# Two loads of 128 KB for each chunk's up and gate weights, with the down weights' load between them

## The chip, the cores and the metric

The kernel runs on one core of one Trainium2 chip. The metric is the device time of one execution in microseconds (us). Five engines work side by side: TensorE (PE, whose weight loads are shown apart as PEld), VectorE (DVE), ScalarE (ACT), GpSimd (POOL) and SyncE (SP), which here issues nearly all transfers from memory (HBM) to the on-chip SBUF.

## The reference, cut to what matters

The input x has 4 sequences of 512 tokens with 512 features. An attention layer comes first, then a recurrent cell (GRU) over the 512 positions, and its states go through a mixture of experts whose result is added to x:

```
x = x + attention(interpolate(x, cond))
h = cond;  for t in 512 steps:                  # GRU, all four sequences at once
    r, z = sigmoid(x[t] W_ih + h W_hh + b)      # first two thirds
    n    = tanh(i_n + r * h_n);  h = (1 - z) n + z h
for every token (2048) and every expert e (16, plus one shared):
    y += weight[token, e] * ((silu(h w1_e^T) * (h w3_e^T)) w2_e^T)
x = x + y
```

All 16 experts are computed for all tokens; the routing weight is zero for most. With the shared one there are 704 (filled up to 768) + 16 * 352 = 6400 hidden units, which is 50 chunks of 128.

## The kernel before, in words

After the attention, `scan_and_ffn` cuts the 512 positions into `NBLK` = 8 blocks of 64 steps. While the scan runs through block b, the feed-forward of block b-1 (256 tokens) is computed in the time that TensorE would otherwise wait. The feed-forward of the last block has nothing beside it: it is the kernel's tail.

One block's feed-forward has `NCH` = 50 chunks. Across the blocks they are numbered n = 50 f + c, 0 to 399. For each chunk:

- `up(f, c)` (L1235) waits for the chunk's up and gate weights in `w13` and does 16 matmuls (L1242), eight with the w=0 half (up, from w1) and eight with the w=1 half (gate, from w3), each half being 4 slices of 128x128 in bf16, used twice. The last adds one to `up_done`.
- ScalarE, VectorE and GpSimd turn this into the hidden units `hid`.
- `down(f, c)` (L1249) does 8 matmuls (L1257) with the chunk's down weights in `w2`. The last adds one to `down_done`.

TensorE's order is written out by hand: for each of the 64 steps, `scan_step` (96 matmuls, L1207) and then so many units of ups and downs as the tables `UPS`, `DOWNS` and `LEFT` say. In the tail it is up, down, up, down, with the down two chunks behind the up (L1327 to L1331).

Weights come from HBM again for every block. `w13` has two slots, `w2` has twelve. SyncE's program (`chunks`, L852) says in which order loads are issued: for chunk n the load of w13 for chunk n+2 (256 KB, L846, `w13_load`), which waits until up(n) is done since it takes its slot; then w2 for chunk n (128 KB, L850, `w2_load`), which waits until down(n-12) is done; and for every fourth chunk, except in the last two blocks, a load of 128 KB of GRU inputs (L842, `gi_load`). Each DMA adds 16 to its slot's semaphore when it has landed. An engine's program is in order: what stands behind a waiting instruction waits too.

Of the kernel before, what the change touches and what calls it, by code (L numbers as in the profile page):

```python
# [5 lines left out]
P = 128  # L6
# [3 lines left out]
KT = D // P  # L10
# [4 lines left out]
NBLK = S // TB  # L15
TOK = B * TB
SCH = -(-SI // P)
NCH = SCH + E * TOPI // P
# [690 lines left out]
def scan_and_ffn(nc, a, ps, x2T, whh, wih, bias, spare, h, gi_dram):  # L709

    with ExitStack() as ctx:
        def sb(name, shape, dt):
            return ctx.enter_context(nc.sbuf_tensor(name, shape, dt))

        def sem(name):
            return ctx.enter_context(nc.semaphore(name))
# [19 lines left out]
        w13 = sb("w13", [P, 2, 2, KT, P], BF16)  # L736
# [28 lines left out]
        w13_in, w2_in = [sem("w13_in0"), sem("w13_in1")], [sem("w2_in%d" % n) for n in range(W2S)]  # L765
# [21 lines left out]
        def need(eng, sem, count):  # L787
            if count > 0:
                eng.wait_ge(sem, count)
# [41 lines left out]
        @block.sync  # L831
        def _(sp):
            for dst, src in ((gwf[:], a["gate"]), (ne[:], a["ne"]), (identf[:], a["identf"]), (owner[:], a["owner"])):
                sp.dma_start(dst, src).then_inc(init_in, 16)

            def send_gates(j):
                sp.wait_ge(g_out, j + 1)
                sp.dma_start(gi_dram[1 + j // M3, :, j % M3], gis[:, j % GIS].rearrange("p b t -> p (b t)")).then_inc(gi_sent[j % GIS], 16)

            def gi_load(blk, m):  # L840
                sp.wait_ge(h_ready, (blk - 1) * TB + 1)
                sp.dma_start(gi[blk % 2][:, m].rearrange("p b t -> p (b t)"), gi_dram[blk, :, m]).then_inc(gi_in[blk % 2], 16)  # L842

            def w13_load(n):
                need(sp, up_done, n - 1)
                sp.dma_start(w13[:, n % 2], a["w13"][n % NCH].rearrange("p (w k i) -> p w k i", w=2, k=KT)).then_inc(w13_in[n % 2], 16)  # L846

            def w2_load(n):
                need(sp, down_done, n - W2S + 1)
                sp.dma_start(w2[:, n % W2S], a["w2"][n % NCH]).then_inc(w2_in[n % W2S], 16)  # L850

            def chunks(f):  # L852
                for c in range(NCH):
                    n = f * NCH + c
                    if n + 2 < NBLK * NCH:
                        w13_load(n + 2)
                    w2_load(n)
                    if c % 4 == 2 and f + 2 < NBLK:
                        gi_load(f + 2, c // 4)

            w13_load(0)
            w13_load(1)
            for j in range(M3, GATES):
                send_gates(j)
            for n in range(GIS):
                sp.wait_ge(gi_sent[n], 16 * ((GATES - M3) // GIS))
            for f in range(NBLK):
                chunks(f)
            sp.wait_ge(out_done, 16 * NBLK)
# [329 lines left out]
        def _(pe):  # L1199
# [34 lines left out]

            def up(f, c):  # L1235
                n, u = f * NCH + c, c % 2
                pe.wait_ge(w13_in[u], (n // 2 + 1) * 16)
                need(pe, up1_done, n - 1)
                for w in range(2):
                    for k in range(KT):  # L1240
                        for s in range(2):
                            mm = pe.matmul(ps[:, UB[u], w * TOK:(w + 1) * TOK], w13[:, u, w, k],  # L1242
                                           hb[:, f % 2, s, k].rearrange("p b t -> p (b t)"),
                                           start=(w + k + s == 0), stop=(k == KT - 1 and s == 1), skip_group_check=True)
                        if w == 1 and k == KT - 1:
                            mm.then_inc(up_done, 1)
                        yield
# [15 lines left out]
            def all_ups(f):  # L1263
                for c in range(NCH):
                    yield from up(f, c)
# [137 lines left out]
```

## Time and profile before

| what | value |
|---|---|
| runs | 2694.81, 2695.28, 2695.60 us; median 2695.28 |
| profiled execution, its own time | 2695.09 us |
| its span, first to last instruction | 2693.3 us |
| mean granted TensorE clock | 0.984 |
| TensorE busy | 2537.0 us, 94% |
| VectorE, GpSimd, ScalarE busy | 69%, 42%, 40% |
| up and gate weights' loads | 400 of 256 KB, median 2.7 us from issue to landing |
| down weights' loads | 400 of 128 KB, median 2.7 us |
| read from HBM | 185.51 MB, 74 GB/s over the span |

The first load of a chunk's weights to matter is at 858 us, when the first up starts; the stretch from 860 to 2540 us is called the main stretch here (scan and feed-forward together), and from 2543 us to the end it is the tail. "Issue" is the moment at which SyncE starts the DMA instruction, "landing" the moment at which its semaphore is full.

### The profile page before, as it was taken

How to read it: one execution, taken by the hardware profiler on the slowest of the kernel's cores; microseconds unless marked ns; L12 is line 12 of the kernel's file. 1: busy time of each engine (PE TensorE's matmuls, PEld its weight loads, DVE VectorE, ACT ScalarE, POOL GpSimd, SP SyncE). 2: the span in 40 equal slices, each digit the busy share in tenths (PEclk: the TensorE clock that was granted, in tenths of full speed). 3: DMA queues.
4: the chain of work that ended last, by engine and by line, in shares of the span. 5: the costliest groups of instructions: out<-in, count | busy, mean ns of one | idle time of the engine just before them, and what ended most of it. 6: DMA issues, size and time to landing. Idle time of an engine off the chain costs nothing.

```text
span 2693.3 us, 159401 instructions
## 1 busy us (share of the span) xinstructions
PE 2537.0 (94%) x69506; PEld 1989.6 (74%) x69506; DVE 1864.9 (69%) x7035; ACT 1077.3 (40%) x3639; POOL 1142.8 (42%) x2962
## 2 busy tenths in 40 slices
PE   5879797879999999999999999999999999999999
PEld 2334343538888888888888888888888888888888
DVE  4647474635666777787787778777777777878622
ACT  4473736263333333333333333333333333333333
POOL 2504030103333555455455545554554555455454
PEclk9899999999999999999999999999999999999999
DMA  4100000001111333333233323333332333233244
GB/s 170 56 3 18 10 10 3 2 14 39 49 49 56 96 99 93 94 95 98 86 99 99 91 84 108 94 98 94 94 98 81 99 100 94 88 89 89 87 151 133
DMA packets 144746, 209.39 MB, mean 78 GB/s; under 512 B 16432, under 2 KB 86320, under 8 KB 143664
## 3 DMA queue, kind: packets, MB, share of 16 engines
q1 hardware_dynamic: 142896, 195.01, 23.6%
q8 instruction: 546, 8.95, 1.4%
q10 hardware_dynamic: 1152, 4.19, 0.4%
q14 instruction: 152, 1.25, 0.1%
HBM read 185.51 MB, written 13.63 MB: 74 GB/s over the span
## 4 chain that ended last, share of the span: by engine, by line
PE 71%; DVE 3%; POOL 1%; issue 1%; ACT 1%; DMA 0%; DVEq 0%; POOLq 0%; ACTq 0%
PE ps L1207 27%; PE ps L1242 24%; PE ps L1257 12%; PE ps L1219 6%; PE ps L1231 2%; POOL hidf L899 1%; DVE turn_n L1088 0%; DVE turn L1091 0%; DVE fresh L1101 0%; DVE hcur L1103 0%; DVE hcur L1106 0%; DVE npre L1094 0%; DMA w<-in_w 0%; ACT cand L995 0%; DVE h L1104 0%
## 5 line engine op out<-in xcount | busy, mean ns | idle before, releaser
L1207 PE MATMUL ps<-whh,hcur 128*32 128x128 f16 x49152 | 792.5, 220 | 25.7 <-DVE hcur L1106 13.1
L1207 PEld LDWEIGHTS ps<-whh,hcur 128*32 128x32 f16 x49152 | 694.3, 97 | 149.8 <-DVE hcur L1106 119.7
L1242 PE MATMUL ps<-hb,w 128*128 128x256 f16 x6400 | 782.3, 273 | 0.4 <-DMA w<-in_w 0.3
L1242 PEld LDWEIGHTS ps<-hb,w 128*128 128x128 bf16 x6400 | 602.8, 98 | 96.2 <-DMA w<-in_w 1.4
L891 POOL COPY hb<-hcur 128x32 f16<-128x32 f16 x512 | 170.3, 333 | 666.3 <-DVE hcur L1106 666.3
L988 ACT ACTIVATE r<-ur 128x16 f32<-128x16 f32 x512 | 110.6, 216 | 828.6 <-DVE ur L1082 828.6
L1257 PE MATMUL ps<-hid,w 128*128 128x256 f16 x3200 | 428.4, 273 | 2.2 <-POOL hid L911 1.8
L1257 PEld LDWEIGHTS ps<-hid,w 128*128 128x128 bf16 x3200 | 312.4, 98 | 39.7 <-issue 3.0
L899 POOL TENSOR_TENSOR hidf<-up 128x256 f32<-128x256 f32 x400 | 292.1, 730 | 99.1 <-POOL hid L911 50.8
L911 POOL TENSOR_TENSOR hid<-hidf,hid 128x256 f16<-128x256 f32 x400 | 269.5, 674 | 61.8 <-ACT hid L984 61.8
L1079 DVE STREAM_TRANSPOSE turn<-ps 128x128 f32<-128x128 f32 x512 | 161.8, 316 | 180.3 <-PE ps L1207 170.7
L488 DVE TENSOR_REDUCE mx<-ps 128x2 f32<-128x256 f32 (+3 forms) x256 | 197.6, 818 | 63.3 <-PE ps L626 62.4
L990 ACT ACTIVATE z<-uz 128x16 f32<-128x16 f32 x512 | 110.4, 216 | 324.9 <-POOL uz L907 324.9
L1073 DVE TENSOR_TENSOR up<-ps,wsb 128x256 f32<-128x256 f32 x352 | 149.5, 425 | 93.5 <-ACT sg L978 92.1
L405 ACT ACTIVATE stage<-ps,cs 128x1024 f32<-128x1024 f32 (+3 forms) x256 | 186.6, 791 | 42.2 <-PE ps L649 35.2
L905 POOL TENSOR_TENSOR zs<-turn 128x16 f32<-128x16 f32 x512 | 113.3, 221 | 204.8 <-DVE turn L1084 201.1
L1088 DVE STREAM_TRANSPOSE turn_n<-ps 128x128 f32<-128x128 f32 x512 | 161.3, 315 | 36.4 <-PE ps L1207 8.5
L978 ACT ACTIVATE sg<-ps 128x256 f32<-128x256 f32 x400 | 150.7, 377 | 69.4 <-PE ps L1242 68.2
L1075 DVE TENSOR_TENSOR up<-ps,sg 128x256 f32<-128x256 f32 x400 | 166.2, 415 | 17.6 <-ACT sg L978 16.7
L1101 DVE TENSOR_TENSOR fresh<-cand,omz 128x16 f32<-128x16 f32 x512 | 89.9, 176 | 114.6 <-ACT cand L995 104.2
L984 ACT CAST hid<-hidf 128x256 f16<-128x256 f32 x400 | 156.0, 390 | 8.5 <-PE ps L1257 6.7
L1084 DVE STREAM_TRANSPOSE turn<-ps 128x128 f32<-128x128 f32 x512 | 156.8, 306 | 3.6 <-PE ps L1207 2.9
(155 smaller groups left out, 3050.9 us busy)
## 6 DMA issues: line engine op xcount, KB each, us to landing
w<-in_w SPq DMA_DIRECT2D x400, 256.0 KB, 2.7
w<-in_w SPq DMA_DIRECT2D x400, 128.0 KB, 2.7
gi_scratch<-gis SPq DMA_DIRECT2D x72, 128.0 KB, 1.7
spare<-gi_scratch SPq DMA_DIRECT2D x36, 128.0 KB, 3.0
gi<-gi_scratch SPq DMA_DIRECT2D x36, 128.0 KB, 2.8
x2T<-in_xT SPq DMA_DIRECT2D x4, 1024.0 KB, 7.0
out<-xo ACTq DMA_DIRECT2D x8, 512.0 KB, 4.3
stage<-in_W_hh SPq DMA_DIRECT2D x1, 3072.0 KB, 11.0
```

The lines of the kernel that those rows point to most:

```text
L405: nc.scalar.activation(prob[:, g % 2, 2 * half:2 * half + 2, tt * P:S], pair(b * 2 * NP + NP + i)[:, :, tt * P:S], ACT.Exp, scale=cs[:, 0: ...
L488: nc.vector.tensor_reduce(mx[:, st, h0:h0 + 2], pair(b * 2 * NP + i)[:, :, 0:(st + 1) * P], AX.X, ALU.max).then_inc(max_done, 1)
L891: nc.gpsimd.tensor_copy(hb[:, blk % 2, :, :, :, t].rearrange("p s k b -> p k s b"), hcur[:].rearrange("p k (s c) -> p k s c", c=HALFC)[:, ...
L899: nc.gpsimd.tensor_tensor(hidf[:], up1[:], up2[:], ALU.mult).then_inc(hidf_done, 1)
L911: nc.gpsimd.tensor_tensor(hid[:, (f * NCH + c) % HIDS, 1], hidf[:], hid[:, (f * NCH + c) % HIDS, 0], ALU.subtract).then_inc(hid_lo, 1)
L1075: nc.vector.tensor_tensor(up1[:], ps[:, UB[c % 2], 0:TOK], sg[:, c % 2], ALU.mult).then_inc(up1_done, 1)
L1079: nc.vector.transpose(turn[:, u, 0, :, 0:COLS], ps[:, RB, 0:P].rearrange("p (k c) -> p k c", c=COLS)).then_inc(r_turned, 1)
L1088: nc.vector.transpose(turn_n[:, :, 0:COLS], ps[:, NB, 0:P].rearrange("p (k c) -> p k c", c=COLS)).then_inc(n_turned, 1)
L1207: mm = pe.matmul(ps[j * COLS:(j + 1) * COLS, bank, 0:P], hcur[:, k], whh[:, s, k, at:at + P], start=(k + s == 0), stop=(k == KT - 1 and s ...
L1219: mm = pe.matmul(ps[:, YB + j % 2, 0:TOK], wih[:, w, m, k], xs[:, q % 2, x, k].rearrange("p b t -> p (b t)"), start=(k + w + x == 0), stop ...
L1242: mm = pe.matmul(ps[:, UB[u], w * TOK:(w + 1) * TOK], w13[:, u, w, k], hb[:, f % 2, s, k].rearrange("p b t -> p (b t)"), start=(w + k + s ...
L1257: mm = pe.matmul(ps[:, YB + d // 2, (d % 2) * TOK:(d % 2 + 1) * TOK], w2[:, n % W2S, d * P:(d + 1) * P], hid[:, n % HIDS, s], start=(c + s ...
```

## The change

Each w13 load is cut into its two halves w=0 and w=1, 128 KB each, and w2's load stands between them. Both halves add 16 to the slot's semaphore, so that `up` waits for 32 for each use of the slot, before its first matmul. Bytes, buffers and all other engines' instructions are the same. There are 400 more DMA instructions.

```diff
-            def w13_load(n):
+            def w13_load(n, w):
                 need(sp, up_done, n - 1)
-                sp.dma_start(w13[:, n % 2], a["w13"][n % NCH].rearrange("p (w k i) -> p w k i", w=2, k=KT)).then_inc(w13_in[n % 2], 16)
+                sp.dma_start(w13[:, n % 2, w], a["w13"][n % NCH][:, w * KT * P:(w + 1) * KT * P].rearrange("p (k i) -> p k i", k=KT)).then_inc(w13_in[n % 2], 16)
...
                     if n + 2 < NBLK * NCH:
-                        w13_load(n + 2)
+                        w13_load(n + 2, 0)
                     w2_load(n)
+                    if n + 2 < NBLK * NCH:
+                        w13_load(n + 2, 1)
...
-            w13_load(0)
-            w13_load(1)
+            for n in range(2):
+                for w in range(2):
+                    w13_load(n, w)
...
-                pe.wait_ge(w13_in[u], (n // 2 + 1) * 16)
+                pe.wait_ge(w13_in[u], (n // 2 + 1) * 32)
```

SyncE's instructions before, in the first block of the feed-forward where down weights begin to wait for a free slot (128x1024 is a w13 load, 128x512 a w2 load, L842 a load of GRU inputs):

```order
L850 DMA w<-in_w 128x512 [waits down_done]
L842 DMA spare<-gi_scratch 128x256 [waits h_ready]
L846 DMA w<-in_w 128x1024 [waits up_done]
L850 DMA w<-in_w 128x512 [waits down_done]
L846 DMA w<-in_w 128x1024 [waits up_done]
L850 DMA w<-in_w 128x512 [waits down_done]
```

The same place after the change (now L846 is 128x512 too, and "x2" is the second half for one chunk and, behind it, the first half for the next):

```order
L850 DMA w<-in_w 128x512 [waits down_done]
L846 DMA w<-in_w 128x512 [waits up_done]
L842 DMA spare<-gi_scratch 128x256 [waits h_ready]
L846 DMA w<-in_w 128x512 [waits up_done]
L850 DMA w<-in_w 128x512 [waits down_done]
L846 DMA w<-in_w 128x512 [waits up_done] x2
L850 DMA w<-in_w 128x512 [waits down_done]
```

The first half stands where the whole load stood; the second has moved behind w2's load and its wait, and L842 behind that. At the end of SyncE's program, in the tail, it is the same without L842. Before:

```order
L846 DMA w<-in_w 128x1024 [waits up_done]
L850 DMA w<-in_w 128x512 [waits down_done]
L846 DMA w<-in_w 128x1024 [waits up_done]
L850 DMA w<-in_w 128x512 [waits down_done] x3
L711 UNCONDITIONAL_BRANCH [waits out_done]
```

After:

```order
L850 DMA w<-in_w 128x512 [waits down_done]
L846 DMA w<-in_w 128x512 [waits up_done] x2
L850 DMA w<-in_w 128x512 [waits down_done]
L846 DMA w<-in_w 128x512 [waits up_done]
L850 DMA w<-in_w 128x512 [waits down_done] x2
L711 UNCONDITIONAL_BRANCH [waits out_done]
```

The last second half, for chunk 399, stands behind w2's load for chunk 397; two loads of w2 follow it, as they followed the whole load.

## Rows read from the trace of the kernel before

**Rows 1.** The page: its span, its chain's shares by engine, the instruction-fetch queue.
```profile
span 2693.3 us, 159401 instructions
...
q8 instruction: 546, 8.95, 1.4%
...
PE 71%; DVE 3%; POOL 1%; issue 1%; ACT 1%; DMA 0%; DVEq 0%; POOLq 0%; ACTq 0%
```

**Rows 2.** Busy time by stretch: from:to, length, busy us (x instructions), clock, DMA share, GB/s.
```profile
860.00:2540.00 1680.00, 1661.96 (x51642) 1416.48 (x51634) 1329.28 (x5697) 618.35 (x2693) 863.32 (x2484) 1.00 0.32 94
2557.00:2681.00 124.00, 124.00 (x1138) 111.14 (x1137) 33.43 (x88) 44.62 (x117) 64.15 (x92) 1.00 0.49 151
```

**Rows 3.** Who PEld waited for, 860 to 2540 us: total us, times, longest.
```profile
PEld ps L1207 <- DVE hcur L1106: 111.3, 442, 1.1
PEld ps L1207 <- issue: 14.9, 47, 1.0
PEld ps L1242 <- DMA w<-in_w: 1.4, 4, 0.6
```

**Rows 4.** Line 1242, whole span: weight loads, and what its engine's idle time ended with.
```profile
L1242 PEld LDWEIGHTS ps<-hb,w x6400: 95/98/99, 858.0 to 2683.9; 128*128 128x128 bf16 x194
...
  DMA w<-in_w: 1.7, 5
```

**Rows 5.** Line 846 (up and gate weights), 860 to 2540 us: ns min/median/max, then landing.
```profile
L846 SPq DMA_DIRECT2D w<-in_w x350: 327/328/333, 862.7 to 2537.9; - x175
...
DMA to landing us min/median/max: 2.5/2.7/4.9
```

**Rows 6.** The same of line 850 (down weights).
```profile
L850 SPq DMA_DIRECT2D w<-in_w x350: 425/438/1985, 863.0 to 2538.2; - x175
...
DMA to landing us min/median/max: 2.4/2.7/4.9
```

**Rows 7.** The same of line 842 (GRU inputs, third in a row).
```profile
L842 SPq DMA_DIRECT2D spare<-gi_scratch x36: 423/432/1690, 874.3 to 2043.0; - x36
L842 SPq DMA_DIRECT2D gi<-gi_scratch x36: 326/432/1545, 1114.5 to 2287.0; - x36
...
DMA to landing us min/median/max: 2.1/2.9/4.9
```

**Rows 8.** Timeline of SyncE at 1410 us: start, duration, instruction.
```profile
1410.67 0.33 SPq L846 DMA_DIRECT2D w<-in_w  x1
1411.04 1.92 SPq L850 DMA_DIRECT2D w<-in_w  x1
1413.01 0.43 SPq L842 DMA_DIRECT2D spare<-gi_scratch  x1
```

**Rows 9.** Timeline of PEld there.
```profile
1412.20 1.35 PEld L1207 LDWEIGHTS ps<-whh,hcur 128*32 128x32 f16 x96 [0.32 <-DVE hcur L1106]
1413.66 1.21 PEld L1242 LDWEIGHTS ps<-hb,w 128*128 128x128 bf16 x12
```

**Rows 10.** Timeline of SyncE in the tail.
```profile
2567.06 0.33 SPq L846 DMA_DIRECT2D w<-in_w  x1
2567.43 0.53 SPq L850 DMA_DIRECT2D w<-in_w  x1
```

**Rows 11.** Timeline of PEld there.
```profile
2565.01 1.74 PEld L1242 LDWEIGHTS ps<-hb,w 128*128 128x128 bf16 x16
...
2567.63 1.74 PEld L1242 LDWEIGHTS ps<-hb,w 128*128 128x128 bf16 x16
...
2570.47 1.74 PEld L1242 LDWEIGHTS ps<-hb,w 128*128 128x128 bf16 x16
```

**Rows 12.** SyncE in the tail: first, largest and last of eight long issues.
```profile
2580.97 1.22 SPq L850 DMA_DIRECT2D w<-in_w  x1
...
2646.47 1.59 SPq L850 DMA_DIRECT2D w<-in_w  x1
...
2674.05 1.09 SPq L850 DMA_DIRECT2D w<-in_w  x1
```

## The prediction

> **What bounds the kernel now.** I read the page's chain first: TensorE has 71% of it and DMA nothing [rows 1]. Then busy time by stretch: 1662 of 1680 us in the main stretch, and every microsecond of the tail, so whatever delays TensorE there is paid in full [rows 2]. Does it wait for anything that would swallow a delay? Before each scan step it waits for the hidden state, 111.3 us in 442 waits, 0.25 each. But in the timeline nearly all of these are the same 0.21 us, which looks like a fixed cost of starting a scan step; only what is above it is slack, and that is 0.04 us a step, some 18 us over the stretch [rows 3]. Last, the wait for weights: 1.7 us in 5 waits over the whole run [rows 4]. Today's loads land 2.7 us after their issue [rows 5], and that is just in time.
>
> **How much time a w13 load has.** It is issued when up(n-2) is done and needed when up(n) begins. In the tail the rows give it: issued at 2567.06, right after the ups that began loading at 2565.01, needed at 2570.47, thus a lead of 3.41 us, and the same for nearly all 49 chunks of the tail [rows 10, 11]. In the main stretch I took each issue of L846 against every 16th weight load of L1242 (400 and 6400, their first and last in [rows 4, 5]). Of the 349 chunks 209 have over 4.8 us, since two scan steps lie in between; 67 have 3.44 to 3.7 (mean 3.55), 62 have 3.7 to 4.1 (mean 3.97), 11 have 4.1 to 4.8.
>
> **The change part by part.**
>
> *The first half* stands where the whole stood, with half the bytes. It lands no later than before. It gains nothing, since a chunk waits for both.
>
> *w2's load* has the same place behind one w13 DMA, with less data ahead. It is used many chunks later in the main stretch; earlier is worth nothing.
>
> *The second half* is now third. An L846 issue takes 0.33 us and w2's begins 0.37 us after it [rows 5, 8, 10]; w2's takes d, at median 0.44 [rows 6]; then 0.05. So the second half is issued at 0.42 + d. No row shows a third load behind 256 KB, but L842 is a 128 KB load that stands third behind 384 KB: from its issue it lands after 2.1 at least and 2.9 at median [rows 7]. I take 2.15, since less is ahead of it. Undisturbed the second half thus lands at 0.42 + 0.44 + 2.15 = 3.0 us against 2.7 now, and 3.41 is enough. No stall.
>
> *But d is not always 0.44.* It reaches 1.99 [rows 6]. In the main stretch every third issue of L850 takes over 0.6 us, with a mean of 1.1; in the tail eight stand out, 0.79, 1.06, 1.07, 1.09, 1.19, 1.22, 1.41 and 1.59, at distances of mostly 13.7 us, that is every fifth chunk [rows 12]. The trace puts many of them down to the wait for down_done, but in the tail down(n-12) was done ten chunks ago. What fits is the instruction-fetch queue: 546 packets of 16 KB, each holding its DMA engine about 1.1 us (1.4% of 16 engines' span) [rows 1], and the trace's packets show one of them in flight beside every long issue. Whatever the cause, today it delays w2, which nobody awaits, and L842. From now on it delays the second half. At 1410.67 it can be seen: w2's issue takes 1.92, the third DMA starts at 1413.01, 2.34 after the first [rows 8]. With 2.15 the second half would land at 1415.2, and up(n) began at 1414.22 (its first load is the sixth of the 12 in [rows 9]): a stall of 0.9 us.
>
> The sum of these: a stall is (0.42 + d + 2.15) - lead.
> Tail: d - 0.84 for each of the eight, 0.22 + 0.23 + 0.25 + 0.35 + 0.38 + 0.57 + 0.75 = 2.8 us.
> Main: 31 of the 67 tightest chunks stand behind a long issue (mean d 1.17); 21 stall, by 9 us together. Of the 62 with about 3.97, six stall, 1.5 us. The 11: 0.5. Together 11 us.
>
> *Late landings without a long issue.* A DMA engine can also be held while the data moves. w2's own landings show these, up to 4.9 us [rows 6]; the second half can't land before w2, being behind it on the same engines. By w2's landings, chunk by chunk, this adds 7.7 us in the main stretch and 2.2 in the tail.
>
> *What is given back.* A stall before up(n) also puts off up(n+1), whose load was issued already, so that the next chunk has that much more. Taking this into account chunk by chunk takes off about 2.5 us. The 18 us of slack in the scan's waits lie mostly in other steps and take off little more.
>
> *Hits on the second half itself.* It stays in flight longer than anything today, and a fetch can begin behind w2's issue. L842 shows how often: against the rule above (from the issue 2.15, or 0.37 after w2's landing), a quarter of its 72 loads landed over 0.4 us later and a tenth over 1.5, up to 4.9 from its issue [rows 7]. Drawn in full for every second half this adds 42 us; not at all, 0. L842 has 128 KB more ahead of it and stands later in the burst, so I take a third to a half, 15 us.
>
> Sum: 14 (long issues) + 10 (late landings) - 3 + 15 = 36 us. The profiled execution took 2695.09 us, 0.2 under the median of the runs; 2695.1 + 36 = 2731 us.
>
> The new DMA instructions themselves (400 of 0.33 us) lie on SyncE, which waits most of the time for up_done. The extra packets (1 KB instead of 2 KB) lie on DMA engines that are busy 32% in the main stretch and 49% in the tail [rows 2]. L842 is now fourth, but its data are needed a block later. If any of these covers went, it would be seen as longer landings, that is rival B.
>
> **Where the skill weighs in.** The rows have 128 KB at 2.7 us from issue [rows 6]. The Trainium skill, DMA: Bandwidth & Descriptors, section on the anatomy of one DMA, gives for GpSimd's path 2.0 us fixed plus bytes over 436 GB/s. For 131 KB that would be an estimate of 2.3 us, so a second half at 0.86 + 2.3 = 3.2 us, still within 3.41, and no stall anywhere: by this formula alone the time stays 2695. The skill's Runtime: NRT & Kernel Launch, section on instruction fetch, says that an engine's instructions come in blocks of 16 KiB and that this is mostly hidden. The 16 KB packets agree; that they cost nothing is what I doubt, since here a load with 0.4 us to spare stands behind them.
>
> **The rivals.**
>
> A, the second half is hidden anyway: the long issues belong to the place behind a 256 KB load, and with 128 KB ahead they shrink. For: L846 alone never issues slowly (327 to 333 ns), the trouble starts behind its 2 KB packets [rows 5]. Against: L842, behind w2, has issues up to 1.69 as well [rows 7]. Time: 2695 to 2700.
>
> B, every third DMA in a burst lands late, as L842's median of 2.9 says. Then an undisturbed second half comes at 0.86 + 2.8 = 3.66, later than 3.41: all the tail's chunks stall by 0.25 (every second one, by the giving back: 6 us) and the 67 tight ones by 0.1, the disturbed ones by 0.65 more. Worked out chunk by chunk this is 55 us without and 106 us with all hits: 2750 to 2800.
>
> C, faster. TensorE waits for "issue" 14.9 us in 47 waits before scan steps [rows 3], perhaps for its own instructions, whose fetch shares DMA engines with 2 KB packets. Smaller packets of 1 KB let a fetch through sooner. Were a third to all of it saved and the second half nearly always in time, the time would be 2680 to 2690. It decides the sign only if the stalls stay under what it saves, and nothing shows that these waits come from w13.
>
> **How the numbers follow.** The forecast (long issues and late landings now reach the weights that TensorE awaits) has 0.68, with its own range of +15 to +60, 2710 to 2755. A has 0.13, B 0.15, C 0.04. The range that holds 8 in 10 takes in the lower half of B and ends above A: 2704 to 2768. What a measurement can tell from no change is 0.2%, 5.4 us. Slower by more: forecast and B and a little of A, 0.85; the same: 0.11; faster: 0.04.
>
> **What would show it.** In the profile after, L1242 waits for "DMA w<-in_w" some 60 to 100 times, 25 to 60 us in total, instead of 1.7; in the tail these waits follow long L850 issues, every fifth chunk. Landing at median stays near 2.5 for both halves. L1207's waits above 0.21 shrink slightly. Busy times stay. It is wrong if L1242's waits stay under 5 us (A), or if nearly every tight chunk waits (B), or if time appears elsewhere while the weights are there.

## The result, and the profile after

Five runs of the changed kernel took 2706.42 to 2715.88 us, median 2710.63; the kernel before, beside it, took 2694.48 to 2695.60, median 2694.81. The ratio is 1.0059, with a 95% interval of 1.0044 to 1.0073: slower by 15.8 us. The forecast was 2731 us. Direction and place were right, the size was not: +36 forecast, +16 measured. The profiled execution took 2709.29 us.

The page after, with span, instruction-fetch queue, and the chain by engine and line (answers to [rows 1]; lines have moved by 3, so that L1245 is the ups' line, L1260 the downs', L1210 the scan's):

```profile
span 2707.5 us, 159801 instructions
...
q8 instruction: 546, 8.95, 1.4%
...
PE 67%; DMA 3%; DVE 3%; issue 1%; SPq 1%; POOL 1%; ACT 1%; DVEq 0%; POOLq 0%; ACTq 0%
PE ps L1210 26%; PE ps L1245 23%; PE ps L1260 11%; PE ps L1222 6%; DMA w<-in_w 3%; PE ps L1234 2%; SPq L850 1%; POOL hidf L902 0%; DVE turn_n L1091 0%; DVE turn L1094 0%; DVE fresh L1104 0%; DVE hcur L1109 0%; DVE hcur L1106 0%; DVE npre L1097 0%; ACT cand L998 0%
```

DMA has gone from 0 to 3% of the chain, and with it SyncE's queue on L850, the issue of w2. That is the forecast's mechanism: the issue of w2, held for longer than its usual 0.44 us, reaches the chain. The list of who PEld waited for over the whole span (engine, line, cause: total us, times, longest), after and then before:

```profile
PEld ps L1210 <- DVE hcur L1109: 111.7, 423, 2.3
PEld ps L1210 <- issue: 29.2, 111, 1.4
PEld ps L1245 <- DMA w<-in_w: 27.1, 58, 1.6
```

```profile
PEld ps L1207 <- DVE hcur L1106: 119.7, 457, 2.3
PEld ps L1207 <- issue: 25.6, 98, 1.0
PEld ps L1242 <- DMA w<-in_w: 1.4, 4, 0.6
```

Waits for weights rose by 25.7 us. The first two rows must be read together. Every scan step's first load has its gap of 0.21 us; when a step comes late, the hidden state has been there for long, and the view calls that gap "issue". 34 waits moved over in this way. The sum of the two rows is 145.3 us before and 140.9 after, 4.4 less.

These rows leave out every gap under 0.15 us, so I also took the matmuls of both traces in order, 69506 in each, and compared the time from one start to the next. From the first up to the end the profiled execution is 13.8 us longer. The ups account for +20.3 us, the scan steps for -6.5, everything else for 0.0. So the change has two effects: waits for weights, which cost 20 us of TensorE's time, and shorter scan steps, which give 6.5 back.

SyncE's loads in the main stretch after the change (answers to [rows 5, 6]):

```profile
L846 SPq DMA_DIRECT2D w<-in_w x700: 327/328/1790, 863.1 to 2548.7; - x175
...
DMA to landing us min/median/max: 1.9/2.3/5.0
```

```profile
L850 SPq DMA_DIRECT2D w<-in_w x350: 328/437/1958, 863.4 to 2548.2; - x175
...
DMA to landing us min/median/max: 2.1/2.4/4.5
```

In these stretches L846 had never been held before (333 ns at most); now its issue, in the third place of the burst, takes up to 1.79 us (a burst is what SyncE issues for one chunk without a wait between). Chunk by chunk over both stretches, w2's issue took over 0.6 us in 103 of 400 cases (132 before), and the second half's in 32: the held issues are as many as before, and spread over two places.

One chunk of the tail shows the whole mechanism. SyncE, PEld and PE after the change (start, duration):

```profile
2617.25 0.33 SPq L846 DMA_DIRECT2D w<-in_w  x1
2617.62 1.19 SPq L850 DMA_DIRECT2D w<-in_w  x1
2618.86 1.34 SPq L846 DMA_DIRECT2D w<-in_w  x2
```

```profile
2620.44 0.21 PEld L1234 LDWEIGHTS ps<-dwT,owner 128*128 128x128 bf16 x2
2621.17 1.64 PEld L1245 LDWEIGHTS ps<-hb,w 128*128 128x128 bf16 x16 [0.52 <-DMA w<-in_w]
```

```profile
2619.68 1.04 PE L1260 MATMUL ps<-hid,w 128*128 128x256 f16 x8
2620.55 0.38 PE L1234 MATMUL ps<-dwT,owner 128*128 128x256 f16 x2
2621.18 1.92 PE L1245 MATMUL ps<-hb,w 128*128 128x256 f16 x16 [0.24 <-DMA w<-in_w]
```

The first half is issued at 2617.25, w2's issue is held for 1.19 us, the second half starts at 2618.86, 1.61 after the first (0.42 + d, as forecast), and the up that could have begun at 2620.66 begins at 2621.17. One thing was not forecast. Normally a matmul starts 0.11 us behind its weight load (2620.44 and 2620.55); after the wait only 0.01 behind it. Of PEld's wait of 0.52 us about 0.1 is taken from this lead, and the matmuls are only 0.41 late. Over all ups it is the same: at the median their first matmul starts 0.107 us behind its load without a wait and 0.004 behind it after one, and the intervals before the ups' first loads grow by 25.6 us, while the ups' matmuls come only 20.3 us later.

### The profile page after: what moved, and what is told of

It reads as the page before. It is cut to its first block, busy times and chain, and to the rows that moved or that the text cites. A ratio compares the mean times of both kernels' runs of the same rounds, so it can differ in the third digit from the quotient of the medians.

```text
span 2707.5 us, 159801 instructions
## 1 busy us (share of the span) xinstructions
PE 2540.3 (94%) x69506; PEld 1983.1 (73%) x69506; DVE 1866.4 (69%) x7035; ACT 1077.0 (40%) x3639; POOL 1140.6 (42%) x2962
## 4 chain that ended last, share of the span: by engine, by line
PE 67%; DMA 3%; DVE 3%; issue 1%; SPq 1%; POOL 1%; ACT 1%; DVEq 0%; POOLq 0%; ACTq 0%
PE ps L1210 26%; PE ps L1245 23%; PE ps L1260 11%; PE ps L1222 6%; DMA w<-in_w 3%; PE ps L1234 2%; SPq L850 1%; POOL hidf L902 0%; DVE turn_n L1091 0%; DVE turn L1094 0%; DVE fresh L1104 0%; DVE hcur L1109 0%; DVE hcur L1106 0%; DVE npre L1097 0%; ACT cand L998 0%
## 5 line engine op out<-in xcount | busy, mean ns | idle before, releaser
L1210 PE MATMUL ps<-whh,hcur 128*32 128x128 f16 x49152 | 787.6, 220 | 24.9 <-DVE hcur L1109 12.5
L1245 PE MATMUL ps<-hb,w 128*128 128x256 f16 x6400 | 789.1, 273 | 12.0 <-DMA w<-in_w 11.0
L1210 PEld LDWEIGHTS ps<-whh,hcur 128*32 128x32 f16 x49152 | 693.2, 97 | 144.9 <-DVE hcur L1109 111.7
L1245 PEld LDWEIGHTS ps<-hb,w 128*128 128x128 bf16 x6400 | 597.7, 98 | 121.7 <-DMA w<-in_w 27.1
L1260 PE MATMUL ps<-hid,w 128*128 128x256 f16 x3200 | 428.3, 273 | 2.2 <-POOL hid L914 1.8
L1260 PEld LDWEIGHTS ps<-hid,w 128*128 128x128 bf16 x3200 | 312.2, 98 | 39.9 <-issue 3.0
L1082 DVE STREAM_TRANSPOSE turn<-ps 128x128 f32<-128x128 f32 x512 | 161.9, 316 | 190.2 <-PE ps L1210 180.9
L1222 PE MATMUL ps<-xs,wih 128*128 128x256 f16 x1344 | 158.9, 274 | 0.0
## 6 DMA issues: line engine op xcount, KB each, us to landing
stage<-in_W_hh SPq DMA_DIRECT2D x1, 3072.0 KB, 11.1
```

Of the source, the lines that this page charges most:

```text
L1082: nc.vector.transpose(turn[:, u, 0, :, 0:COLS], ps[:, RB, 0:P].rearrange("p (k c) -> p k c", c=COLS)).then_inc(r_turned, 1)
L1210: mm = pe.matmul(ps[j * COLS:(j + 1) * COLS, bank, 0:P], hcur[:, k], whh[:, s, k, at:at + P], start=(k + s == 0), stop=(k == KT - 1 and s ...
L1222: mm = pe.matmul(ps[:, YB + j % 2, 0:TOK], wih[:, w, m, k], xs[:, q % 2, x, k].rearrange("p b t -> p (b t)"), start=(k + w + x == 0), stop ...
L1260: mm = pe.matmul(ps[:, YB + d // 2, (d % 2) * TOK:(d % 2 + 1) * TOK], w2[:, n % W2S, d * P:(d + 1) * P], hid[:, n % HIDS, s], start=(c + s ...
```

## The experiments

Each ratio is against the kernel before, run beside on the same chip. In these later runs the kernel before itself scattered more than in the first ones (2686 to 2699 us), so ratios are compared, not times. Single traces scatter too: the two of the kernel before differ by 3.1 us from the first up to the end, all of it in the scan steps. "Stops" are short gaps between two weight loads inside a scan step for which the trace has no releaser.

**Both kernels again**, for a second pair of traces, from another set of runs.

> The kernel before, unchanged, for a trace from the chip on which the next three run. Two-part theory (the change adds waits for the second half and takes away a part of the short stops inside a scan step, in which TensorE has no instructions): about 50 to 60 such stops, 14 to 16 us together, and under 2 us of waits for weights. If the stops are a property of one chip, there are half as many here or none.

> The changed kernel, unchanged, beside the kernel before on the same chip. Two-part theory: 60 to 90 waits for weights of 25 to 30 us, stops inside scan steps down by a quarter to two thirds from those of the kernel before on this chip, and a ratio of 1.003 to 1.007 (+8 to +19 us). Lateness theory alone: +20 us or more, the stops as before.

The kernel before: 2692.19 us, ratio 0.9999 (0.9988 to 1.0009). The changed kernel: 2705.80 us, ratio 1.0051 (1.0035 to 1.0067). PEld's waits before:

```profile
PEld ps L1207 <- DVE hcur L1106: 120.2, 459, 2.3
PEld ps L1207 <- issue: 21.5, 85, 1.0
```

And after:

```profile
PEld ps L1210 <- DVE hcur L1109: 111.7, 423, 2.4
PEld ps L1245 <- DMA w<-in_w: 29.0, 51, 1.7
PEld ps L1210 <- issue: 23.0, 100, 1.0
```

The change is confirmed on a second set of runs, and so are both parts: waits for weights +27.7 us (1.3 before), the sum of the scan line's two rows 141.7 before and 134.7 after, 7.0 less. Matmul by matmul, the ups add 23.5 us and the scan steps take away 10.5, together 13.0. Counted load by load inside the scan steps of the main stretch, the stops over 0.03 us were 59 of 15.6 us and 57 of 12.4 us in the two traces of before, 33 of 11.1 and 24 of 4.5 in those of after. Most of them had stood in the profile as "issue" [rows 3]. They are paid in full: in the first trace of before, a scan step with stops is longer than one without by their sum and 0.04 us. Of the expectations, the ratio, the total of the waits and the fall of the stops held; 51 waits are fewer than the 60 to 90 expected, and 12.4 us of stops before are a little under the 14 to 16.

**The same loads, half a chunk more time.** Each half has its own semaphore, and TensorE waits for the second before the ninth matmul.

```diff
-                pe.wait_ge(w13_in[u], (n // 2 + 1) * 32)
                 need(pe, up1_done, n - 1)
                 for w in range(2):
+                    pe.wait_ge(w13_in[u][w], (n // 2 + 1) * 16)
```

> The changed kernel's loads in the changed order, but each half has its own semaphore, and TensorE waits for the second half only before the chunk's ninth matmul, 0.87 us later. Lateness theory: the second half has a lead of 4.28 instead of 3.41 us, which covers even an issue held by 1.6 us; the first half lands at 2.3 us. 0 to 10 waits, 2693 to 2697 us. Rival, splitting itself: 2705 or above.

2684.48 us, ratio 0.9972 (0.9960 to 0.9983). Its waits:

```profile
PEld ps L1210 <- DVE hcur L1109: 121.0, 460, 2.3
PEld ps L1210 <- issue: 15.4, 66, 0.6
PEld ps L1245 <- DMA w<-in_w: 0.2, 1, 0.2
```

Same DMAs, same order, and the loss is gone: it was TensorE's wait for the second half and nothing else. It is even 7 us faster than before, under the expected range, which had no term for the stops. "Issue" is 15.4 us against 25.6 and 21.5 in the two traces of before: the stops have gone down and nothing stands against it now.

**A third slot, split and whole.** w13 gets three slots and every load is issued one chunk earlier.

```diff
-        w13 = sb("w13", [P, 2, 2, KT, P], BF16)
+        w13 = sb("w13", [P, 3, 2, KT, P], BF16)
...
-                need(sp, up_done, n - 1)
+                need(sp, up_done, n - 2)
```

> The changed kernel's loads in the changed order, but w13 has three slots and each load is issued one chunk earlier. Lateness theory: the lead grows by one chunk, 2.6 us in the tail and about 4.8 in the main stretch, so no chunk waits; the time is that of the kernel before less the 1.7 us of weight waits it has: 2692 to 2695 us. Rival, splitting itself (more DMA work in the way of the instruction fetches or of TensorE's reads): it stays at +10 us or more, 2705 or above.

> The split loads with three slots again, on the same chip as its whole-load twin. Two-part theory: 4 to 7 us of stops inside scan steps, no waits for weights, -5 to -8 us against the kernel before and 3 to 7 us under the twin with whole loads. Rival: equal to the twin within 1 us.

> The kernel before (loads of 256 KB) with three w13 slots, each load issued one chunk earlier. No chunk waits for its weights. Two-part theory: the stops inside scan steps stay (10 to 16 us), since the 2 KB packets stay; -1 to -3 us against the kernel before. Rival, it is not the split but the waits removed or the longer lead that made the split kernel with three slots 6 us faster: -5 to -8 us, as that one.

Split: 2685.23 us, ratio 0.9973 (0.9962 to 0.9985), and again 2684.40, 0.9976 (0.9966 to 0.9985). Whole: 2691.55 us, 0.9999 (0.9990 to 1.0008). None waits for weights. The waits of the split one (second run), then the whole one:

```profile
PEld ps L1210 <- DVE hcur L1109: 121.1, 460, 2.3
PEld ps L1210 <- issue: 15.3, 65, 1.1
```

```profile
PEld ps L1208 <- DVE hcur L1107: 120.7, 461, 2.4
PEld ps L1208 <- issue: 21.8, 83, 1.3
```

The first expectation (2692 to 2695 us) was missed: it knew only the waits for weights, and the kernel came out 7 us under it. The second held, and the third for the stops (11.4 us stay); its time is -0.3 us where -1 to -3 was expected. The twins differ in the loads alone, in their cut and in w2's place, and by 7 us in time. Matmul by matmul they differ by 7.7 us from the first up on, all of it in the scan steps. So split loads in this order are by themselves a gain of 6 to 7 us, and more lead for whole loads gains nothing. The rival of splitting as a cost falls.

**Both halves in a row**, w2 behind them.

> Both halves are issued in a row, and w2's load behind them. Lateness theory (the time goes where TensorE waits for the second half, which starts too late behind w2's issue): the second half is now second in the burst, so it lands as w2's load did in the kernel before, mostly 3.1 us after the first issue and up to 3.9 when its issue is held. About 45 waits, and +5 to +10 us, that is 2700 to 2705 us. Rival, splitting itself (400 more DMA instructions, 1 KB packets in place of 2 KB): as the changed kernel, +14 to +18 us. Rival, position alone: +0 to +2 us.

> Both halves in a row with w2 behind them and one wait for both, again, on the same chip as the other three. Two-part theory: 15 to 30 waits of 4 to 9 us in all, stops 5 to 7 us, -2 to -6 us against the kernel before.

2687.97 us, 0.9982 (0.9971 to 0.9993), and again 2687.58, 0.9984 (0.9976 to 0.9993): faster than before, where the first expectation said 5 to 10 us slower. 5.7 and 3.0 us of waits for weights, "issue" 18.4 and 18.2. The expectation for the first run had counted the waits too high (45; they were 19) and left out the stops. The one for the second, made with both, held for the time (-3.6 us) and the stops (7.0 us), but not for the waits: 10 of 3.0 us, where 15 to 30 of 4 to 9 us were expected. Against the changed kernel this is the price of w2's place between the halves: some 18 us.

With a wait of its own for each half as well:

> Both halves issued in a row, w2 behind them, each half with its own semaphore and TensorE waiting for the second only before the ninth matmul of the chunk. Two-part theory: no waits for weights (lead of the second half 4.28 us, landing at 2.6 to 3.9), stops inside scan steps 4 to 6 us: -6 to -9 us against the kernel before, the same as with w2 between them within 2 us. If the order of w2 matters for the stops, the two differ by more.

2685.31 us, 0.9979 (0.9970 to 0.9987), -5.9 us and so just short of the -6 to -9 expected; "issue" 16.0: as the one with w2 between them, within the intervals. Where TensorE has the time, w2's place costs nothing that these runs can tell.

**Whole loads, w2 ahead.** First try, with only the two lines exchanged:

> w13's load is whole again (256 KB), but issued behind w2's. Lateness theory: it is issued 0.42 + d after up(n-2) is done (d is how long w2's issue takes, 0.44 at median) and takes 0.4 us longer than a half to land, about 3.3 us in all when nothing disturbs, against a lead of 3.41 in the tail and 3.45 to 3.7 for 67 chunks of the main stretch. 80 to 110 waits and +23 to +32 us, 2718 to 2727 us. Rival, splitting itself: no split, so +0 to +3 us.

2690.60 us, 0.9996 (0.9987 to 1.0004): a miss, and a mistake in the edit. w2's load now had no wait ahead of it and was issued behind the last w13 load, one chunk early; SyncE's order in time was as before:

```profile
2601.66 0.33 SPq L846 DMA_DIRECT2D w<-in_w  x1
2602.03 1.40 SPq L850 DMA_DIRECT2D w<-in_w  x1
2604.28 0.33 SPq L846 DMA_DIRECT2D w<-in_w  x1
```

Second try, with w2 waiting for up(n-2) too:

```diff
                     if n + 2 < NBLK * NCH:
-                        w13_load(n + 2)
+                        need(sp, up_done, n + 1)
                     w2_load(n)
+                    if n + 2 < NBLK * NCH:
+                        w13_load(n + 2)
```

> w13's load is whole (256 KB) and issued behind w2's, with w2's load now also waiting for up(n-2), so that both leave together (in the earlier kernel w2's had no wait ahead of it and left one chunk earlier, so nothing had changed for w13's). Lateness theory: a w13 load starts 0.42 + d after up(n-2) is done and lands at 3.3 us undisturbed; 80 to 110 waits, 25 to 40 us in all, stops inside scan steps as in the kernel before: +20 to +33 us. Rival, only the split matters: within 3 us of before.

2707.74 us, ratio 1.0064 (1.0052 to 1.0077), +16.5: again less than the +20 to +33 expected. Its waits:

```profile
PEld ps L1209 <- DVE hcur L1108: 114.4, 434, 2.3
PEld ps L1209 <- issue: 24.2, 100, 1.2
PEld ps L1244 <- DMA w<-in_w: 23.5, 40, 1.2
```

So no split is needed for the loss; it is enough that what TensorE awaits is issued behind w2. The waits are 40 of 23.5 us, where 80 to 110 of 25 to 40 were expected. The stops, 8.8 us here, are 3 us fewer than in the second trace of before although nothing is split; that is no more than two traces of one kernel differ by.

**A larger dose.** The changed kernel with w2 in two loads of 64 KB, both between the halves.

> The changed kernel with w2's load also cut into two (64 KB each), both between the halves of w13, so that the second half is fourth in the burst, issued 0.48 us later still. Lateness theory with the sizes as measured: 90 to 160 waits, 40 to 60 us in all, of which 0.1 us each is absorbed: +25 to +50 us. Rival, the position counts for nothing and only instruction stops do: under +16 us.

2742.05 us, ratio 1.0194 (1.0181 to 1.0208), +51. The waits:

```profile
PEld ps L1212 <- DVE hcur L1111: 102.1, 382, 2.3
PEld ps L1247 <- DMA w<-in_w: 71.2, 108, 1.9
PEld ps L1212 <- issue: 30.5, 137, 1.0
```

A delay of the issue by some 0.5 us makes 71 us of waits from 27 to 29, more than the 40 to 60 expected, and the time is just above the expected range: the leads of the changed kernel end just where its landings begin.

**What of the split removes the stops?** Two ways to halve something, with three slots so that no chunk waits.

```diff
-                sp.dma_start(w13[:, n % 3, w], ...
+                sp.dma_start(w13[w * 64:(w + 1) * 64, n % 3], ...       # two DMAs, 2 KB packets
```

```diff
-        w13 = sb("w13", [P, 3, 2, KT, P], BF16)
+        w13 = sb("w13", [P, 3, 2, KT + 1, P], BF16)                     # one DMA, 1 KB packets
```

> Three slots and the changed order, but the w13 load is cut into partitions 0 to 63 and 64 to 127, so that the two loads of 128 KB have packets of 2 KB as the whole load has. Packet-size theory (the stops inside scan steps come from 2 KB packets in the way of the instruction fetch): stops as with whole loads, PEld's waits at the scan line put down to issue 20 to 26 us, and -0 to -2 us against the kernel before. Two-loads theory (it is the cut into two DMAs, whatever the packets): 15 to 18 us of such waits and -5 to -8 us.

> Three slots and one load of 256 KB for each chunk, but w13's slot has a hole behind each half, so that the packets are 1 KB. Packet-size theory: stops as in the split kernels, 15 to 18 us of waits at the scan line put down to issue, and -5 to -8 us. Two-loads theory: 20 to 26 us and -0 to -2 us.

Halves by partition: 2696.37 us, ratio 1.0014 (1.0005 to 1.0023), where both theories had expected it no slower than before. One load in 1 KB packets: 2706.44 us, 1.0056 (1.0042 to 1.0070). Their "issue" rows:

```profile
PEld ps L1210 <- issue: 25.7, 92, 2.2
```

```profile
PEld ps L1208 <- issue: 34.7, 112, 1.4
```

Both theories fall: neither change does it alone, and the second makes it much worse. Both together (15.3 us) are better than neither (21.8). Why is left open. The single load in 1 KB packets also has a longer issue, 0.55 instead of 0.33 us, and another layout in SBUF, so packet size is not its only difference. But these runs, none of which waits for weights, settle that the stops are time: "issue" of 15.3, 21.8, 25.7 and 34.7 us goes with 1822.7, 1830.4, 1834.4 and 1845.4 us from the first up to the end. Against the whole loads that is -7.7, +4.0 and +14.9 us, and the scan steps have -7.9, +3.9 and +14.9 of it.

## Why the prediction was wrong in size

*What bounds the kernel, and the lead of 3.41 us:* right. Waits for weights come where the lead is short, 51 of the main stretch and 16 of the tail (counted chunk by chunk); a third slot removes all.

*The second half is issued at 0.42 + d, and d is at times long:* right. Its issue came 0.85 us after the first's at median. Its landing took 2.37 us at median from its own issue, against the 2.15 that I took from L842's shortest. The held issues are those beside an instruction-fetch packet, as I had read in the rows: so it is for 131 of the 132 of w2 in the trace of before.

*The sum of waits, 14 + 10 - 3:* nearly right. *The hits, 15 us:* this is the first mis-sized term, and the largest. Chunk by chunk, the trace after has 27.6 us of waits. My rule for the landing (2.15 us from the issue, or 0.37 behind w2's landing) gives 18.8 of them, landings up to 0.4 us later than the rule add 5.3, and the hits, those over 0.4 us later, add 3.5. In the second pair the same parts are 19.1, 4.4 and 6.2. Hits are rarer than the rows of L842 said: 17% of second halves land over 0.4 us later than the rule and 5% over 1.5 (19% and 7% in the second pair), against a quarter and a tenth. And of the 68 in the first trace, 50 fall on chunks with a lead over 4.8 us and only 7 on chunks that wait. The forecast had 36 us more of waits, the rows have 25.7: this takes 10 off.

*Each microsecond of wait is paid in full:* not quite, and this is the second. I had looked only for slack in the scan steps. TensorE's loads run 0.1 us ahead of its matmuls, which absorbs 0.1 of each wait: 58 waits, 5 to 6 us.

*Rival C, fewer stops without an instruction:* this is the third, a term that I left out of the sum. To it I gave 0.04, as a case of its own that needed the stalls to be nearly absent. It goes with every run whose halves are w=0 and w=1, and shortens the scan steps by 6.5 us in the first pair, 10.5 in the second (0.9 of each is ahead of a step's first matmul, where a step that comes late waits less for the hidden state). The reason that I gave, smaller packets, is not borne out: one load in 1 KB packets makes the stops worse.

Together: 36 - 10 - 5 - 7 = 14 us, which is what the two profiled executions differ by (14.2); the medians differ by 15.8. The rows alone, without the gaps under 0.15 us, give 25.7 - 5.8 - 4.4 = 15.5 for the first pair and 27.7 - 5.1 - 7.0 = 15.6 for the second, whose spans differ by 13.3.

*In the tail* the first up began at 2553.03 and the end came 154.5 us later, 4.3 more than before; I had 2.8 + 2.2 and a share of the hits.

*Rival A* fails with the 27 us of waits; *rival B* too, as not every tight chunk waits (51 waits in the main stretch, which has 129 chunks with a lead under 4.1 us). The three covers I named (SyncE's time, busier DMA engines, L842 as fourth) held.

The two split versions with no waits, 0.9972 and 0.9976, beat both kernels.

## What to carry to other kernels

When a load's landing is close to its use, what is issued ahead of it on its queue is part of its latency, the times included at which that issue is held; read the longest duration of an issue, not its median, against the lead. Cutting a load costs nothing only if the part that lands last is still in time, by more lead or because the consumer waits for each part where it needs it. And price a change's good side effects as terms of the sum, not only as a rival.

## What the runs showed of the hardware

SyncE's DMA issues behind another are at times held, up to 2 us, while a 16 KB packet of the instruction-fetch queue is in flight. In the trace of before 132 issues of w2 took over 0.6 us; 131 of them had such a packet beside them, and at the median they ended 0.37 us after it. Of the 268 shorter ones 47 had one beside them. Of the 32 long issues of second halves in the trace after, 21 had one; for the other 11 the cause is not shown.

After each of the 58 stops over 0.06 us inside scan steps in the first trace of before, the next weight load begins 1.2 to 1.6 us after such a packet has ended, while the packets start 3.9 us apart at median. So it looks as if TensorE's instructions arrive just in time here, and as if the way in which the weights are loaded delays some of them: the stops in the main stretch sum to 4.5 us with two loads of 128 KB and three slots, and to 25 us with one load in 1 KB packets. That they are waits for the fetched instructions is inferred from this timing; no run changed the fetch itself. The packets of the main stretch take the same time in all five runs with three slots, 1.06 to 1.09 us on average, so they are not slower; what makes the instructions late stays open.

A load of 256 KB takes SyncE 0.33 us to issue with 128 packets of 2 KB and 0.55 with 256 of 1 KB, and lands 0.4 us later, at 3.1 us:

```profile
L846 SPq DMA_DIRECT2D w<-in_w x400: 545/546/703, 602.7 to 2688.2; - x134
```

The changed kernel's time scatters more than that of the kernel before in the first set (9.5 us against 1.1). In the second set the two scatter alike (6.8 us against 7.9 in its run beside it), so this is not shown to come from the change.
